# Expert up projection of an MoE layer with the weights held stationary and fetched per tile

## The reference

```python
logits = flat @ router_w.T + router_b
topk_vals, topk_idx = jax.lax.top_k(logits, 2)
topk_w = jax.nn.softmax(topk_vals, axis=-1)
for e in range(8):
    cw = jnp.sum(jnp.where(topk_idx == e, topk_w, 0.0), axis=-1)
    y = jax.nn.gelu(flat @ w1[e].T + b1[e], approximate=False)   # 256 -> 1024
    y = y @ w2[e].T + b2[e]                                      # 1024 -> 256
    out = out + y * cw[:, None]
```

## Time and profile before

| | us |
|---|---|
| median of three runs (778.06 to 779.0) | 778.6 |
| span of the profiled execution | 776.3 |
| TensorE matmul busy in it | 620.4 (80%) |
| VectorE, ScalarE, GpSimd busy | 355.6, 187.6, 170.2 |
| stage of the slot tiles, first up to last down | 379 to 719 |
| DMA traffic, mean | 59 GB/s |

### The profile page before, as it was taken

The page is one execution under the profiler, slowest core; times in us unless marked ns, Lnnn a source line. Parts: engine busy times, 40 slices in busy tenths (PEclk is TensorE's granted clock), DMA queues, the critical chain, the costliest instruction groups (busy, mean ns, idle before and its releaser), DMA issues.

```text
span 776.3 us, 9245 instructions
## 1 busy us (share of the span) xinstructions
PE 620.4 (80%) x2756; PEld 435.1 (56%) x2757; DVE 355.6 (46%) x835; ACT 187.6 (24%) x357; POOL 170.2 (22%) x215
## 2 busy tenths in 40 slices
PE   3548988997899889931699999999999999999000
PEld 1226765776577678831366666666666666666000
DVE  1744783676567463238332332233223322332395
ACT  2004322423332243100122222223222222222022
POOL 1110110101110110010123333333433343333441
PEclk9859898979897896555599999999999999999655
DMA  8920000100010070018112111211121112111402
GB/s 259 378 65 1 1 28 0 55 1 28 0 54 0 0 305 1 0 53 299 68 20 34 34 27 27 34 34 27 27 34 34 27 27 34 34 27 28 135 33 76
DMA packets 33513, 45.56 MB, mean 59 GB/s; under 512 B 3851, under 2 KB 29784, under 8 KB 33112
## 3 DMA queue, kind: packets, MB, share of 16 engines
q1 hardware_dynamic: 25960, 34.99, 13.2%
q0 software_dynamic: 7536, 10.36, 8.3%
HBM read 33.81 MB, written 11.53 MB: 58 GB/s over the span
## 4 chain that ended last, share of the span: by engine, by line
PE 62%; DVE 18%; DMA 5%; issue 4%; ACT 3%; POOL 1%; DVEq 1%; POOLq 0%; ACTq 0%
PE psum_a L1137 16%; PE psum_v L1146 14%; PE psum_b L942 7%; PE psum_v L1029 6%; PE psum_b L1155 4%; PE psum_a L1008 4%; PE psum_c L1019 3%; DVE ln_stats L553 3%; PE psum_m L1046 2%; PE psum_b L949 2%; DMA sums<-work,add_rows 2%; DMA work<-x_rows,load_rows 1%; DVE score_max L691 1%; PE psum_b L994 1%; DVE ln_mdiff L558 1%
## 5 line engine op out<-in xcount | busy, mean ns | idle before, releaser
L1137 PE MATMUL psum_a<-expert_w,work 128*128 x312 | 146.9, 614 | 9.0 <-issue 8.1
L1146 PE MATMUL psum_v<-expert_w,work 128*128 x624 | 141.2, 379 | 0.9 <-DVE work L863 0.9
L857 DVE TENSOR_TENSOR work<-psum_a,front_weights_then_b 128x512 f32<-128x512 f32 x78 | 50.5, 687 | 199.4 <-DMA sums<-work,add_rows 186.1
L1146 PEld LDWEIGHTS psum_v<-expert_w,work 128*128 128x128 f32 x624 | 118.5, 190 | 33.4 <-issue 19.3
L531 ACT ACTIVATE work<-work 128x512 f32<-128x512 f32 x78 | 48.0, 631 | 245.6 <-DVE work L857 245.6
L1137 PEld LDWEIGHTS psum_a<-expert_w,work 128*128 128x128 f32 x312 | 57.1, 193 | 74.9 <-issue 74.4
L344 POOL TENSOR_TENSOR ln_rstd<-ln_veps,minus_half 128x4 f32<-128x4 f32 x20 | 21.0, 1049 | 257.3 <-DVE ln_veps L566 257.3
L942 PE MATMUL psum_b<-expert_w,front_weights_then_b 128*128 128x512 f32 x128 | 71.5, 706 | 4.3 <-ACT expert_w L447 1.7
L1029 PEld LDWEIGHTS psum_v<-front_weights_then_b,work 77*128 77x128 f32 x512 | 73.9, 222 | 1.7 <-ACT work L478 0.9
L1029 PE MATMUL psum_v<-front_weights_then_b,work 77*128 77x17 f32 (+1 forms) x512 | 73.7, 279 | 0.7 <-ACT work L478 0.7
L393 POOL DMA_INDIRECT sums<-work,add_rows x38 | 61.0, 1606 | 31.1 <-POOL add_rows L408 31.1
(11 more groups left out here) (155 smaller groups left out, 665.0 us busy)
## 6 DMA issues: line engine op xcount, KB each, us to landing
expert_w<-in_w SPq DMA_DIRECT2D x16, 1024.0 KB, 11.9
front_weights_then_b<-in_b SPq DMA_DIRECT2D x1, 2560.0 KB, 15.8
expert_w<-in_x SPq DMA_DIRECT2D x4, 512.0 KB, 3.8
x_rows<-x SPq DMA_DIRECT2D x4, 512.0 KB, 3.0
sums<-x SPq DMA_DIRECT2D x4, 512.0 KB, 4.1
expert_w<-sums SPq DMA_DIRECT2D x4, 512.0 KB, 5.4
out<-expert_w SPq DMA_DIRECT2D x4, 512.0 KB, 2.9
front_weights_then_b<-in_b SPq DMA_DIRECT2D x1, 1536.0 KB, 13.0
```

Source lines behind the costliest of these rows:

```text
L857: dve.tensor_tensor(hb[:, n * 512:(n + 1) * 512], pa[:, n, :], b1_s[:, bass.ds(e, 1), n * 512:(n + 1) * 512].rearrange("p a f -> p (a f)") ...
L1137: last = pe.matmul(pa[:, n, :], xtT[:, k, :], w1_v[:, bass.ds(e, 1), k, n * 512:(n + 1) * 512].rearrange("p a f -> p (a f)"), start=(k == ...
L1146: last = pe.matmul(pv[:, 0:D], hgT[:, k, :], w2_v[:, bass.ds(e, 1), k, :].rearrange("p a d -> p (a d)"), start=(k == 0), stop=(k == KF - 1))
```

## The change

`up` is turned round: a 128 x 128 block of `w1[e]` is held stationary and the tile's 128 rows (`xtT`) stream through it, 16 matmuls of 128 columns, each recorded as two pieces. The result stands in PSUM with the 1024 hidden features on the partitions, so the bias is one number per partition: ScalarE applies bias and gelu in one instruction per block of 128 features, eight a tile, from PSUM into `hidT`, which `down` takes as it is. The adds of b1 on VectorE, `turn_hidden` and both copies go. `pa` and `pb` take turns as up's output.

w1 no longer stays in SBUF: the host packs each expert's blocks and its bias columns into one array `w1b`, and SyncE fetches 128 x 2056 numbers (1.05 MB) for each tile into a ring of three (`w1_ring`), each when the gelu of three tiles before has been made. w2 stays in SBUF, loaded after the second chunk of x. b2 and the norm weights are loaded at the end of the front.

`xt`, `xtT`, `hidT` and `yt` are double. The loops are unrolled, the index columns are used without a copy. TensorE's order becomes `up(t)`, `turn_rows(t + 1)`, `down(t - 1)`. GpSimd's order becomes `load_tile(t + 2)`, `add_tile(t)`; it also makes the four `base` additions of the tail in between, before the adds of tiles 4, 8, 12 and 16. VectorE keeps the two steps after `down`.

The diff, cut: renamed semaphores, the layout of SBUF and those lines of the tile loops that the listing above shows are left out.

```diff
+W1_ROW = KD * FF + KF
+RING3 = 3
...
+        w1_ring = [FRONT[:, n * W1_ROW:(n + 1) * W1_ROW] for n in range(RING3)]
+        at_front = RING3 * W1_ROW
+        hidT = [FRONT[:, at_front + n * FF:at_front + (n + 1) * FF].rearrange("p (c q) -> p c q", c=KF) for n in range(2)]
+        at_front += 2 * FF
+        xt = [FRONT[:, at_front + n * D:at_front + (n + 1) * D] for n in range(2)]
+        at_front += 2 * D
+        xtT = [FRONT[:, at_front + n * D:at_front + (n + 1) * D].rearrange("p (k q) -> p k q", k=KD) for n in range(2)]
+        at_front += 2 * D
+        yt = [FRONT[:, at_front + n * D:at_front + (n + 1) * D] for n in range(2)]
+        assert at_front + 2 * D <= 12 * 1024
...
@@ sync @@
-            for e in range(EARLY):
-                sp.dma_start(w1_v[:, e], w1[e].rearrange("(k p) f -> p k f", p=P)).then_inc(experts_in, 16)
-                sp.dma_start(w2_v[:, e], w2[e].rearrange("(k p) d -> p k d", p=P)).then_inc(experts_in, 16)
...
+            for e in range(E):
+                sp.dma_start(w2_v[:, e], w2[e].rearrange("(k p) d -> p k d", p=P)).then_inc(w2_in, 16)
...
-            sp.wait_ge(xt_mm, 1)
-            sp.dma_start(R[:, 3840:5888], b2.rearrange("e d -> (e d)").partition_broadcast(P)).then_inc(b2_in, 16)
-            sp.wait_ge(y_ready, SLOT_TILES)
+            sp.dma_start(LATE[:, 0:E * D], b2.rearrange("e d -> (e d)").partition_broadcast(P)).then_inc(b2_in, 16)
             sp.dma_start(lnw_s, lnw.partition_broadcast(P)).then_inc(ln_in, 16)
             sp.dma_start(lnb_s, lnb.partition_broadcast(P)).then_inc(ln_in, 16)
+            sp.wait_ge(table_ready, 1)
+            for t in range(SLOT_TILES):
+                e = nc.values_load(expert_of[0:1, t:t + 1], engines=[mybir.EngineType.SP], min_val=0, max_val=E - 1,
+                                   skip_runtime_bounds_check_because="the table is clamped to the experts")
+                if t >= RING3:
+                    sp.wait_ge(hT_made, 2 * (t - RING3) + 2)
+                sp.dma_start(w1_ring[t % RING3], w1b[bass.ds(e, 1)].rearrange("a p f -> p (a f)")).then_inc(w1_in[t % RING3], 16)
...
@@ gpsimd @@
-            def load_tile(idx):
-                pool.indirect_dma_start(xt, None, x2_dram, bass.IndirectOffsetOnAxis(idx, 0)).then_inc(xt_in, 16)
-            def add_tile(idx):
-                pool.indirect_dma_start(sums, bass.IndirectOffsetOnAxis(idx, 0), yt, None,
+            def load_tile(t):
+                if t >= 2:
+                    pool.wait_ge(xt_mm, t - 1)
+                pool.indirect_dma_start(xt[t % 2], None, x2_dram,
+                                        bass.IndirectOffsetOnAxis(token_of[:, t:t + 1], 0)).then_inc(xt_in[t % 2], 16)
+            def add_tile(t):
+                pool.wait_ge(y_ready, t + 1)
+                if t >= 1:
+                    pool.wait_ge(y_out, 16 * t)
+                pool.indirect_dma_start(sums, bass.IndirectOffsetOnAxis(sum_of[:, t:t + 1], 0), yt[t % 2], None,
                                         compute_op=ALU.add).then_inc(y_out, 16)
-            pool.wait_ge(table_ready, TABLES)
-            pool.wait_ge(x2_out, (2 * CHUNKS + 1) * 16)
-            load_tile(token_of[:, 0:1])
-            pool.wait_ge(xt_mm, 1)
-            load_tile(token_of[:, 1:2])
-            with pool.Fori(1, SLOT_TILES) as t:
-                pool.wait_ge(xt_mm, t + 1)
-                pool.tensor_copy(load_rows[:, :], token_of[:, bass.ds(t + 1, 1)]).then_inc(load_set, 1)
-                pool.wait_ge(x2_out, (2 * CHUNKS + 1) * 16)
-                pool.wait_ge(load_set, t)
-                load_tile(load_rows[:, :])
-                pool.wait_ge(y_ready, t)
-                pool.tensor_copy(add_rows[:, :], sum_of[:, bass.ds(t - 1, 1)]).then_inc(add_set, 1)
-                pool.wait_ge(x2_out, (2 * CHUNKS + 1) * 16)
-                pool.wait_ge(add_set, t)
-                add_tile(add_rows[:, :])
-            pool.wait_ge(y_ready, SLOT_TILES)
-            add_tile(sum_of[:, SLOT_TILES - 1:SLOT_TILES])
-            pool.wait_ge(xt_in, 16 * XS_TILES)
             def base(g):
                 pool.tensor_tensor(fin[:, g * CT:(g + 1) * CT, :], X2[:, g * CT:(g + 1) * CT, :],
                                    lnb_s.rearrange("p (j d) -> p j d", j=1).to_broadcast([P, CT, D]),
                                    ALU.add).then_inc(base_ready, 1)
+            pool.wait_ge(table_ready, TABLES)
+            pool.wait_ge(x2_out, (2 * CHUNKS + 1) * 16)
+            load_tile(0)
+            load_tile(1)
+            pool.wait_ge(ln_in, 2 * 16)
+            for t in range(SLOT_TILES):
+                if t + 2 < SLOT_TILES:
+                    load_tile(t + 2)
+                if t in (4, 8, 12, 16):
+                    base(t // 4 - 1)
+                add_tile(t)
...
-                base(g)
...
@@ scalar @@
+            def turned_rows(t):
+                act.wait_ge(xt_mm, t + 1)
+                act.activation(xtT[t % 2], pm[:, 0:D].rearrange("p (k q) -> p k q", k=KD), ACT.Copy).then_inc(xt_ready, 1)
+            def hidden(t):
+                src = (pa, pb)[t % 2]
+                bias = w1_ring[t % RING3][:, KD * FF:W1_ROW]
+                if t >= 2:
+                    act.wait_ge(y_mm, t - 1)
+                for n in range(2):
+                    act.wait_ge(h_mm, 2 * t + n + 1)
+                    for c in range(n * KF // 2, (n + 1) * KF // 2):
+                        q = c - n * KF // 2
+                        last = act.activation(hidT[t % 2][:, c, :], src[:, n, q * P:(q + 1) * P], ACT.Gelu,
+                                              bias=bias[:, c:c + 1])
+                    last.then_inc(hT_made, 1)
             act.preload_act_table(ACT.Gelu)
+            turned_rows(0)
+            for t in range(SLOT_TILES):
+                hidden(t)
+                if t + 1 < SLOT_TILES:
+                    turned_rows(t + 1)
...
@@ vector @@
+            dve.wait_ge(b2_in, 16)
+            for t in range(SLOT_TILES):
+                e = nc.values_load(expert_of[0:1, t:t + 1], engines=[mybir.EngineType.DVE], min_val=0, max_val=E - 1,
+                                   skip_runtime_bounds_check_because="the table is clamped to the experts")
+                if t >= 2:
+                    dve.wait_ge(y_out, 16 * (t - 1))
+                dve.wait_ge(y_mm, t + 1)
+                dve.tensor_tensor(yt[t % 2], pv[:, 0:D], b2_s[:, bass.ds(e, 1), :].rearrange("p a d -> p (a d)"),
                                   ALU.add).then_inc(yb_ready, 1)
+                dve.wait_ge(yb_ready, t + 1)
+                dve.tensor_scalar(yt[t % 2], yt[t % 2], weight_of[:, t:t + 1], None, ALU.mult).then_inc(y_ready, 1)
...
@@ tensor @@
+            def turn_rows(t):
+                pe.wait_ge(xt_in[t % 2], (t // 2 + 1) * 16)
                 for k in range(KD):
+                    last = pe.transpose(pm[:, k * P:(k + 1) * P], xt[t % 2][:, k * P:(k + 1) * P], ident[:, :])
                 last.then_inc(xt_mm, 1)
+            def up(t):
+                dst = (pa, pb)[t % 2]
+                w1 = w1_ring[t % RING3][:, 0:KD * FF].rearrange("p (k f) -> p k f", k=KD)
+                pe.wait_ge(w1_in[t % RING3], (t // RING3 + 1) * 16)
                 pe.wait_ge(xt_ready, t + 1)
                 for n in range(2):
+                    if t >= 2:
+                        pe.wait_ge(hT_made, 2 * (t - 2) + n + 1)
+                    for q in range(KF // 2):
+                        c = n * KF // 2 + q
+                        for k in range(KD):
+                            last = pe.matmul(dst[:, n, q * P:(q + 1) * P], w1[:, k, c * P:(c + 1) * P], xtT[t % 2][:, k, :],
+                                             start=(k == 0), stop=(k == KD - 1))
                     last.then_inc(h_mm, 1)
+            def down(t):
+                e = nc.values_load(expert_of[0:1, t:t + 1], engines=[mybir.EngineType.PE], min_val=0, max_val=E - 1,
+                                   skip_runtime_bounds_check_because="the table is clamped to the experts")
+                if t >= 1:
+                    pe.wait_ge(yb_ready, t)
+                for c in range(KF):
+                    if c % (KF // 2) == 0:
+                        pe.wait_ge(hT_made, 2 * t + c // (KF // 2) + 1)
+                    last = pe.matmul(pv[:, 0:D], hidT[t % 2][:, c, :], w2_v[:, bass.ds(e, 1), c, :].rearrange("p a d -> p (a d)"),
+                                     start=(c == 0), stop=(c == KF - 1))
                 last.then_inc(y_mm, 1)
             pe.wait_ge(table_ready, 1)
+            pe.wait_ge(w2_in, E * 16)
+            turn_rows(0)
+            for t in range(SLOT_TILES):
+                up(t)
+                if t + 1 < SLOT_TILES:
+                    turn_rows(t + 1)
+                if t >= 1:
+                    down(t - 1)
+            down(SLOT_TILES - 1)
...
@@ host @@
+    w1_rows = turned(a("ffn_w1").reshape(E, FF, KD, P), 0, 3, 2, 1).reshape(E, P, KD * FF)
+    b1_cols = turned(a("ffn_b1").reshape(E, KF, P), 0, 2, 1)
```

(51 more changed lines are left out.)

94 lines of the change are left out of this document (21 added, 73 removed).

## The result

| | before | after |
|---|---|---|
| median, us | 778.7 (778.1 to 779.0) | 856.9 (847.1 to 865.9) |
| profiled execution, us | 778.6 | 860.65 |
| its span, us | 776.3 | 858.6 |

The change makes the kernel slower: ratio 1.096, 95% interval 1.078 to 1.114. On a second chip the same two kernels gave 767.0 and 865.4 us, ratio 1.123 (1.114 to 1.132). Each ratio compares the faster executions of both kernels, so it differs a little from that of the medians. The forecast was 835 us, with a range of 806 to 885.

A forecast was written before the change was run, and what follows sets the result against it. TensorE bound the tile stage, GpSimd's loop nearly ending last. Span 776.3 us with +52.2 - 1.9 - 6.1 = +44.2 gave 820.5; +12 for the clock 832.5, plus 2.3 the forecast 835 us, range 806 to 885.

The forecast's parts named there:

- the sum without clock falls: Whole kernel: span 820.5 us, from +52.2 - 1.9 - 6.1 = +44.2 on the span before.
- The central step: GpSimd's queue: the next load waits behind the add, loop 5.91 us, interval 10.13 against 8.60, TensorE idle some 2.4.
- The table read: TensorE before down: reading the expert with only two transposes to hide it, 0.5 us, between 0 and 1.24.
- Up: TensorE's up: 32 pieces of 128 columns take 3.55 us, at most 4.2, costing nothing to speak of.
- The clock: Tile stage: idle stretches lower the clock in one interval of five, 7 x 1.7 = +12 us, between 0 and 63.
- rival 2: Tile stage: same loop, but the clock falls in nearly every interval, 63 us on 820.5, 886 us; chance 0.16.
- The start: Before up(0): the first gather meets a w1 load, +1.5 us (0 to 2.1).
- The front: Before the tiles: w2, b2 and norm weights load earlier and nothing waits for them, 0 us.
- The ends: Last two tiles without gather waits, 760.0 to 771.5 us; last add -1.9 us, base additions out of the tail -6.1.
- the first: Tile stage: the gather is hidden, TensorE's 7.22 us set the interval, 722 us, faster; chance 0.05.
- The third: Tile stage: w1 traffic meets the gathers, 36 x 2.1 = 76 us on 820.5, 899 us; chance 0.05.
- The fourth: TensorE's up: weight loads stand between its pieces, up 9.6 us, interval 13.8, total 966 us; chance 0.01.

The follow-up runs named there:

- the two experiments that undid it in different ways: Changed kernel with a third row buffer and gathers issued one add earlier, 721.6 us; changed kernel with two buffers, rows turned after down, 740.8 us.
- the early read: Changed kernel with TensorE's read of down's expert moved ahead of the transposes of rows: 844.3 us in one execution.
- the kernel without fetches: The version with three row buffers, but w1 fetched for the first three tiles only: 721.9 us, ratio to before 0.944.

## Why the prediction was right, and by how much it was off

The time, 856.9 for 835, lies in the range, and its mechanism was the forecast's. Point by point, against the profiled span of 858.6 where the sum without clock falls was 820.5:

*The central step* held: the load cannot pass the waiting add, TensorE idles before the transposes of rows, and the two experiments that undid it in different ways gave 7.25 and 8.02 us. The loop from down's end to the landing was 0.38 + 0.81 + 0.28 + 1.89 + 2.8 = 6.16 us for 5.91. The one term that no row had shown, a gather right behind an add, costs 1.89 and not 1.60: 0.3 us of issue lie between. From the landing to down it was 0.02 + 0.57 us for 0.77, and down itself 3.55 for 3.45 (514.86 to 518.41). The undisturbed interval is 10.31 for 10.13. Over 36 intervals: +6.5 us.

*The table read*, taken at 0.5 us between 0 and 1.24, is 0.35: 0.57 from the transposes of rows to down less their 0.22, and the early read took 0.30 to 0.35 of it away.

*Up* at 3.55 us was right (3.57 with three row buffers), its loads hidden, as were ScalarE's eight pieces (four in 1.14 us, under down and up).

*The clock* is the step that was mis-sized. Its price was right, its count was not. The 36 intervals took 415.1 us; at 10.31 each they would be 371.2, and late gathers account for 7.4 (their landings over 2.8 us, summed). The rest, 36.5 us for 21 downs at the low clock, is 1.74 us each, forecast 1.7. The forecast put one down in five at the low clock, 12 us; it was three in five. In count the truth lay between the forecast (7) and rival 2 (all). The second chip agrees: 25 downs at the low clock, (421.6 - 371.2 - 7.6) / 25 = 1.71. The rows could not have given the count: in the tile stage before, up to its last tile, there was no idle stretch over 0.43 us to learn from, and the earlier trace rows showed one fall, not how often.

*The late gathers* (+7.4) were missed. They were there to see: the median of the gathers was read the earlier trace rows and not their spread, since they were hidden before.

*The start.* From the first gather's issue to up(0) it was 7.8 us (360.19 to 368.02) against 4.4 (374.85 to 379.25), +3.4 for the forecast +1.5 (0 to 2.1). The first gather meets three w1 loads of 1 MB, not one as in the earlier trace rows, and lands after 6.5 us. By the end of the first down another 0.5 us was lost.

*The front* was counted at nothing and came out 14.7 us shorter (last router product at 329.5 for 344.2). That is no effect of the change but of the clock: other kernels with this very front had 344 and 347, and the kernel before with GpSimd's loop unrolled, whose front is that of the kernel before, had 329.6. It went the other way than the clock in the tile stage and hid two fifths of its 36.5 us. This was luck: with the front at 344.2 the span would have been 873.3 us, still inside the range, but 41 above the forecast's 832.5 and not 26.

*The ends.* From down 36 to the last down 11.5 us for 11.5; from the last down's end to the end of the program 48.9 for 49.0. The last add took 5.3 us from down's end to landing (809.71 to 815.02) for 5.31, and no VectorE operation in the tail stands for 2 us, which putting the base additions back prices at 6.1 us for 6.1.

Sum: 820.5 - 14.7 + 1.9 + 0.5 + 6.5 + 7.4 + 36.5 = 858.6.

Of the rivals, the first (TensorE's 7.22 us set the pace, 722 us) did not happen in the changed kernel, but the third row buffer makes it happen: 7.25 us and 721.6. The third is refuted by the changed kernel's own landings, 2.8 us in the median as before, with the same seven late ones; the kernel without fetches adds that the fetches themselves delay nothing. The fourth is refuted by up's 3.57 us. Rival 2 had the right mechanism and too high a count. What stays open is why in the changed kernel one tile falls and the next, with the same 2.5 us of idle time ahead of it, does not.

## What to carry to other kernels

Two buffers overlap nothing when the load that fills the second stands in an in-order queue behind an instruction that waits for the consumer. Before a queue's order is fixed, write down for each load what stands ahead of it, what that waits for, and how much work lies between that event and the load's use; here issuing the loads one tile further ahead, in an edit that also added a third buffer, took the interval from 11.53 to 7.25 us and turned a loss of 10% into a gain of 6%. And an idle stretch in TensorE has two prices: itself, and the low clock behind it. At 2.45 us in each 10.3 us the second added two fifths of the first (36.5 us over 36 tiles, 1.0 beside the 2.45).

## What the runs showed of the hardware

The same front took between 326 and 347 us, by the time that TensorE worked in it at the low clock: 64 us of work in the shortest, 108 in the longest. The windows view of one stretch in two kernels with identical instructions up to there, three row buffers with fetches and without:

```profile
292.00:316.00 24.00, 21.05 (x143) 17.64 (x142) 11.36 (x30) 8.10 (x18) 0.00 (x0) 0.91 0.00 1
```

```profile
292.00:316.00 24.00, 24.00 (x112) 20.69 (x111) 7.98 (x21) 6.03 (x13) 0.00 (x0) 0.59 0.00 1
```

At a mean clock of 0.91 TensorE gets through 143 pieces in 24 us, at 0.59 through 112. The two spans, 701.3 and 719.6 us, differ by 18.3, and the fronts, 326.2 and 344.1, by 17.9. The spread of the kernel before, 760 to 779 us over two chips, goes the same way: the mean granted clock was 0.881 in its execution of 760.1 us and 0.858 in those of 778 to 779 on the same chip. The front of the kernel before ended at 344.2 us in its own profile and at 329.6 in that of the kernel with the unrolled loop. A difference under 20 us between two single executions of these kernels has to be read by stage and not from the total.

A gather of 128 rows of 1 KB lands after 2.8 us, in the changed kernel after 3.6 to 4.0 in the last tiles, where empty slots all read one row, and after 6.5 beside three loads of 1 MB. An add and a gather that follow each other on GpSimd start 1.89 us apart, of which 1.58 are the add itself.
